# A Mamba prelude with fewer steps between the engines, and a side softmax that starts at step 5

## The reference, cut to what matters

```python
xs, z = split(u @ in_proj_w.T)                        # 256 + 256 channels
xs = silu(causal_conv4(xs, conv_w) + conv_b)          # 4 taps along the tokens
dt, B, C = split(xs @ x_proj_w.T, [64, 16, 16])
dt = softplus(dt @ dt_proj_w.T + dt_proj_b)
h = h * exp(dt * A) + (dt * xs) * B                   # a scan over the tokens, 16 states a channel
y = sum_over_states(h * C);  y = (y + D * xs) * silu(z);  out = y @ out_proj_w.T
```

## Time and profile before

| | us |
|---|---|
| median of three runs | 1351.88 |
| the three runs | 1352.38, 1351.88, 1346.26 |
| the profiled execution | 1346.07 |
| its span in the profile | 1344.3 |
| from the last block of X1 to the first drive | 62.63 to 154.72 |
| mean granted clock of PE over the span | 0.947 of full |

### The profile page before, as it was taken

How to read it: one execution, slowest core, us unless ns; L and a number is a source line. 1 busy time by engine, 2 the same in 40 slices (tenths; PEclk the granted TensorE clock), 3 DMA queues, 4 the chain that set the end, 5 groups by cost and what they waited for, 6 DMA issues and landing times.

```text
span 1344.3 us, 14496 instructions
## 1 busy us (share of the span) xinstructions
PE 1169.9 (87%) x4978; PEld 617.1 (46%) x4978; DVE 972.0 (72%) x1393; ACT 798.7 (59%) x1097; POOL 549.8 (41%) x291
## 2 busy tenths in 40 slices
PE   5677599999988798999658999999999999797888
PEld 1231144444433343444435666666566666432554
DVE  4557899999986435325668999999899999623353
ACT  4454666666645324222657888888888888534542
POOL 8000288888850655453002545445445454500000
PEclk8879599999998899999869999999999999998999
DMA  3000255555531211111000000000000000000000
GB/s 117 0 2 8 94 183 189 180 191 182 187 129 68 70 34 39 39 41 28 0 2 14 21 15 15 21 14 21 15 14 21 15 15 15 1 0 0 1 1 32
DMA packets 30825, 68.35 MB, mean 51 GB/s; under 512 B 6072, under 2 KB 11736, under 8 KB 30488
## 3 DMA queue, kind: packets, MB, share of 16 engines
q1 hardware_dynamic: 30752, 67.43, 15.4%
HBM read 65.18 MB, written 1.44 MB: 50 GB/s over the span
## 4 chain that ended last, share of the span: by engine, by line
DVE 38%; PE 38%; ACT 17%; issue 5%; POOL 1%; DMA 0%; DVEq 0%; POOLq 0%; SPq 0%; ACTq 0%
DVE work L585 10%; DVE work L1412 6%; DVE work L1431 5%; ACT ps L487 5%; PE ps L880 5%; PE ps L1066 4%; PE ps L896 3%; PE ps L888 3%; ACT work L1273 3%; DVE yd L1476 3%; ACT work L1268 3%; PE ps L1107 2%; DVE work L1479 2%; PE ps L1675 1%; PE ps L1575 1%
## 5 line engine op out<-in xcount | busy, mean ns | idle before, releaser
L1540 POOL TENSOR_TENSOR ssum<-ssum,rs 128x1024 f32<-128x1024 f32 x32 | 77.1, 2408 | 221.3 <-DVE work L1412 219.0
L585 DVE TENSOR_TENSOR_SCAN work<-ps,work 128x1024 f32<-128x1024 f32 x64 | 146.6, 2290 | 8.8
L605 POOL TENSOR_TENSOR work<-work 128x1024 f32<-128x1024 f32 x43 | 102.5, 2383 | 116.7 <-DVE work L585 116.7
L1412 DVE SCALAR_TENSOR_TENSOR work<-work,w_t 128x1024 f32<-128x1024 f32 x96 | 123.3, 1285 | 24.2 <-ACT work L1273 21.9
L870 POOL TENSOR_TENSOR work<-work,ssum 128x1024 f32<-128x1024 f32 x32 | 77.0, 2406 | 127.7 <-DVE work L955 79.3
L409 PE MATMUL ps<-work,ident 128*128 128x512 f32 x256 | 123.0, 604 | 2.5 <-POOL work L605 2.4
L955 DVE TENSOR_TENSOR work<-work,ps 128x512 f32<-128x512 f32 x64 | 43.9, 687 | 109.4 <-PE ps L888 109.2
L487 ACT ACTIVATE ps<-work,A 128x1024 f32<-128x1024 f32 x64 | 71.6, 1119 | 83.3 <-DVE work L585 81.8
L934 ACT ACTIVATE work<-ps 128x512 f32<-128x512 f32 x64 | 38.1, 597 | 131.2 <-PE ps L880 131.2
L1548 POOL TENSOR_TENSOR yd<-yd,work 128x896 f32<-128x896 f32 x32 | 67.1, 2096 | 69.7 <-DVE work L1479 69.7
L1455 DVE SCALAR_TENSOR_TENSOR work<-work,ps 128x64 f32<-128x64 f32 x384 | 79.3, 275 | 6.2
(11 more groups left out here) (342 smaller groups left out, 2604.4 us busy)
## 6 DMA issues: line engine op xcount, KB each, us to landing
work<-bc_rows SPq DMA_DIRECT2D x43, 512.0 KB, 3.6
yd<-bc_rows SPq DMA_DIRECT2D x21, 512.0 KB, 3.7
rs<-w_rows SPq DMA_DIRECT2D x32, 256.0 KB, 3.4
ssum<-share_rows SPq DMA_DIRECT2D x32, 256.0 KB, 3.0
w_t<-in_tile_w SPq DMA_DIRECT2D x32, 195.5 KB, 2.4
work<-in_w SPq DMA_DIRECT2D x1, 2048.0 KB, 8.0
shared<-in_f SPq DMA_DIRECT2D x3, 512.0 KB, 5.8
work<-in_x SPq DMA_DIRECT2D x4, 256.0 KB, 3.5
```

The source lines that it names most:

```text
L585: dve.tensor_tensor_scan(h, flat_pair(DABANK), h, 0.0, ALU.mult, ALU.add).then_inc(m0["scan"], 1)
L605: pool.tensor_tensor(HS[u % 4], HS[u % 4], CB[u % 3], ALU.mult).then_inc(m0["state"], 1)
L1412: c = dve.scalar_tensor_tensor(HC[u], HP[:, tap:tap + SEQ], par(u, "taps", tap), HC[u], ALU.mult, ALU.add)
L1540: pool.tensor_tensor(ssum[:, b, :], ssum[:, b, :], rs[:, :, :].rearrange("p k t -> p (k t)"), ALU.add).then_inc(m2["ss"], 1)
```

## The change

In the prelude: the peak of X1 is reduced block by block. The top-2 moves behind norm 2 (`f0_route_dve`), and its result is turned by 2 transposes instead of 16, evicted as 128x256, stored by SP in two DMAs (indicators and weights), and the indicators are loaded back. ACT writes the last tap of the convolution along with each eviction. `x_proj` is one product per block for dt, B and C. The bias of dt is a 65th row of `dt_proj` against a row of ones that POOL writes. Softplus is one function with its own table. POOL makes the middle and low parts of B. The four blocks go in two pairs, with the engines' lists interleaved. In the expert loop the plan `SOFT` is moved by `LAG` = 5 steps (5, 7, 9, 11, 15, 17, 19, 21), with all that hangs on it; gates(0), ups(0) and two gate blocks move too.

```diff
 def l0_clip_dve, per block k:
+    dve.wait_ge(m0["dve"], m0["x1"] + k + 1)
+    dve.tensor_reduce(gam[:, 0, 2 * k:2 * k + 2], blk(X1, k).rearrange("p (g t) -> p g t", t=GL), AX.X, ALU.max,
+                      apply_absolute_value=True).then_inc(m0["group_peak"], 1)
 def f0_dve, at its end:
-            top2(dve, own, rw[:, 0], rt[:, :, 0:E])
-            dve.tensor_tensor(rt[:, :, E:2 * E], rw[:, 0], rt[:, :, 0:E], ALU.mult).then_inc(f0["dve"], 1)
             l0_factor_dve(dve, own)
+        def f0_route_dve(dve, own):            # called after norm_dve(2)
+            dve.wait_ge(f0["dve"], f0["probs_out"] + 1)
+            top2(dve, own, rw[:, 0], rt[:, :, 0:E])
+            ind, w = (t.rearrange("p (e i) -> p i e", i=NT) for t in by_expert0)
+            dve.tensor_copy(ind, rt[:, :, 0:E])
+            dve.tensor_tensor(w, rw[:, 0], rt[:, :, 0:E], ALU.mult).then_inc(f0["dve"], 1)
 def l0_act, projection evictions:
+                        act.activation(pad[...], ps[:, 4 + m, :], ACT.Copy)
+                        act.activation(DL[:, MI * b + m, h * BL:(h + 1) * BL], ps[:, 4 + m, :], ACT.Identity,
+                                       scale=V("conv_w", m * DC + DC - 1), bias=V("conv_b", m)).then_inc(m0["act"], 1)
+            f0_turn_act(act)
+            gate_xs(0); gate_xs(1); low_out(0); low_out(1); gate_xs(2); rows_out(0); rows_out(1); gate_xs(3)
+            act.preload_act_table_set("softplus")
+            soft_plus(0); soft_plus(1); low_out(2); low_out(3); rows_out(2); rows_out(3)
+            soft_plus(2); soft_plus(3)
             act.preload_act_table_set("natural_log_exp_and_others")
+            def soft_plus(k):
+                act.wait_ge(m0["dtp"], k + 1)
+                act.activation(DL[:, MI * b:MI * (b + 1), h * BL:(h + 1) * BL], pair(4 + MI * (k % 2)), ACT.Softplus).then_inc(m0["delta"], 1)
 def l0_pe, after the projection:
+            f0_turn_pe(pe)
+            project_x(0); project_x(1); project_dt(0); project_dt(1)
+            project_x(2); project_x(3); project_dt(2); project_dt(3)
 def l0_dve, after norm_dve(2):
+            f0_route_dve(dve, own)
+            convolve(0); convolve(1); convolve(2); high_part(0); high_part(1); convolve(3)
+            high_part(2); high_part(3); step_x(0); step_x(1)
+            def high_part(k):
+                own(dve.tensor_copy(blk(parts[64:96, :], k), src))
+                if k >= 2:
+                    dve.wait_ge(m0["b_lo"], k - 1)
+                dve.tensor_tensor(bc_rest[:, k % 2, :], src, blk(parts[64:96, :], k), ALU.subtract).then_inc(m0["bc"], 1)
 def l0_pool:
+            pool.memset(dt_low[DR:DR + 1, :], 1.0).then_inc(m0["dt_ones"], 1)
+            for k in range(NB):
+                tb = part_tmp[0:32, k % 2, :]
+                pool.wait_ge(m0["bc"], k + 1)
+                own(pool.tensor_copy(tb, bc_rest[:, k % 2, :]))
+                pool.tensor_copy(blk(parts[32:64, :], k), tb)
+                pool.tensor_tensor(blk(parts[0:32, :], k), bc_rest[:, k % 2, :], tb, ALU.subtract).then_inc(m0["b_lo"], 1)
 SP, before it loads rows of C:
+            sp.wait_ge(m0["delta"], NB)
+            sp.wait_ge(m0["b_lo"], NB)
 expert loop:
-        SOFT = {j: 2 * j + 2 * (j // NB) for j in range(2 * NB)}
+        SOFT = {j: LAG + 2 * j + 2 * (j // NB) for j in range(2 * NB)}
-                if k == 1:
+                if k == NB - 2:
                     gates(0)
-                if k == 2:
+                if k == NB - 1:
                     ups(0)
-            pe.wait_ge(m1["dve"], m1["sub"] + 1)
-            l1_side_pe(pe, 0)
-                if n in (N1 - 4, N1 - 2):
+                if n in (N1 - 3, N1 - 1):
                     gate_block(...)
```

More of the change, by code:

```diff
@@ L203, in build @@
         norm = sems("norm", NORM)
[L204 to L207, removed]
+        m0 = stages("m0", pe="up:8 down:4 proj:16 outp:4",
+                    act="sign:3 biased:8 evac:16 sum_out:4",
+                    dve="weff:1 gated:8 x1:4 peak:1 scaled:4 ygate:4 s_out:4",
+                    each="gamma xd dtp group_peak dt_ones xs xd_out conv bc b_lo delta dtx b_mm c_out c_rows c_in0 c_in1 c_in2 ysum decay drive scan state")
         f0 = stages("f0", pe="logit:4 probs_T:1 picked_T:1 vT:1 mix:4", act="lg:4 exps:2 v_out:1 g:4",
-                    dve="top:2 probs:2 probs_out:1 picked:1 v:1 x_out:4", each="rt_out rows w_in0 w_in1 h1 h2 h3 r1 r2 r3 pooled summed")
+                    dve="top:2 probs:2 probs_out:1 picked:1 v:1 x_out:4", each="rt_out rows ind_in w_in0 w_in1 h1 h2 h3 r1 r2 r3 pooled summed")
         m1 = stages("m1", pe="logit:1 gq:2 gk:2 comb:2 s:4", act="exps:1 s_out:4",
@@ L374, in l0_pe, with project_x @@
                               start=True, stop=True).then_inc(m0["pe"], 1)
-            for k in range(NB):
+            f0_turn_pe(pe)
+            def project_x(k):
                 b, h = divmod(k, NB // BATCH)
-                pe.wait_ge(m0["act"], m0["xs"] + MI * (b + 1))
-                if k >= 2:
[L379 to L387, removed]
@@ new lines, in project_x, with project_dt @@
+                for m in range(MI):
+                    mm = pe.matmul(ps[0:DR + 2 * DS, k, :], W["x_proj"][:, m * (DR + 2 * DS):(m + 1) * (DR + 2 * DS)],
+                                   XS[:, MI * b + m, h * BL:(h + 1) * BL], start=(m == 0), stop=(m == MI - 1))
+                mm.then_inc(m0["xd"], 1)
+            def project_dt(k):
+                pe.wait_ge(m0["xd_out"], k + 1)
+                if k == 0:
+                    pe.wait_ge(m0["dt_ones"], 1)
+                    pe.wait_ge(m0["act"], m0["evac"] + 2 * MI * NB)
+                if k >= 2:
+                    pe.wait_ge(m0["delta"], k - 1)
+                for m in range(MI):
+                    mm = pe.matmul(ps[:, 4 + MI * (k % 2) + m, :], W["dt_proj"][:, m * P:(m + 1) * P], blk(dt_low, k), start=True, stop=True)
+                mm.then_inc(m0["dtp"], 1)
@@ L467, in l0_act @@
-            act.preload_act_table_set("natural_log_exp_and_others")
-            for k in range(NB):
-                for m in range(MI):
-                    n = MI * k + m
-                    act.wait_ge(m0["pe"], m0["dtp"] + n + 1)
-                    if n >= 2:
-                        act.wait_ge(m0["dve"], m0["delta"] + n - 1)
-                    t = tmp4[:, n % 2, :]
-                    own(act.activation(t, ps[:, 4 + n % 4, :], ACT.Abs, bias=V("dt_b", m)))
-                    own(act.activation(t, t, ACT.Exp, scale=-1.0))
-                    act.activation(t, t, ACT.Ln, bias=1.0).then_inc(m0["act"], 1)
@@ L571, in l0_dve @@
-            dve.wait_ge(m0["dve"], m0["delta"] + MI * NB)
-            dve.wait_ge(m0["pe"], m0["dtp"] + MI * NB)
-            for j in range(BATCH * MI):
-                dve.tensor_tensor(DX[:, j, :], DL[:, j, :], XS[:, j, :], ALU.mult).then_inc(m0["dve"], 1)
-            dve.wait_ge(m0["dve"], m0["dtx"] + BATCH * MI)
+                for i in range(DC - 1):
+                    c = dve.scalar_tensor_tensor(DL[:, j, :], pad[:, j, i:i + SEQ], V("conv_w", m * DC + i),
+                                                 DL[:, j, :], ALU.mult, ALU.add)
+                    if i < DC - 2:
+                        own(c)
```

170 lines of the change are left out of this document (93 added, 77 removed).

## The result

The changed kernel takes 1311.33 us (median of four runs, 1308.02 to 1315.25) against 1350.85 (four runs, 1346.26 to 1352.38) of the kernel before: ratio 0.9714, 95% interval 0.9678 to 0.9750. The forecast was 1316, range 1305 to 1331. The profiled execution took 1311.09 for a span of 1309.4, where before had 1346.07 and 1344.3: 34.9 us less in the span, against a forecast of 33.2.

The account below looks back on a forecast made before the run. No engine is full: the prelude is bound by engines handing blocks on, the expert loop by PE waits and low clock. 25.4 + 7.8 = 33.2 us gives 1312.9; halfway toward the median's 5.8 offset, 1316, range 1305 to 1331.

Parts of the forecast that it names:

- Steps 1 and 2: Prelude, X1 peak to factor: block reduces and top-2 off the path together gain 3.4 us (1.5 to 5.3).
- Step 1: Prelude, peak of X1: four reduces over 512 columns replace one over 2048; gain 1.6 us.
- Step 2: Prelude, top-2 off the path: factor then waits for POOL's all-reduce, starting at 66.8 (64.9 to 68.7) instead of 70.24.
- Step 3: Norm 2: transposes and table load out of the way gain 1.1 us, less 0.7 (0 to 2) for PE's low clock.
- Steps 4 to 7: Projection, convolutions, softplus, POOL and queues: first drive at 133.1 instead of 154.72, 21.6 us, including gains before the projection.
- The rule on the table load: ACT before softplus: a table switch of 2.66 us with drain would take 1.4 us more off the gain.
- The rule of exclusion: Prelude: fourth convolution's taps and step_x may each wait for POOL; 1 us taken on the path, 7.6 for six waits.
- Step 8: Expert loop, side softmax five steps later: 14.9 less 7.7 plus 0.6 for later gates, gain 7.8 us (5 to 10).
- Contention and clock eating a third: Prelude: all-reduce 1.9, norm 2 clock 1.3, projection clock 3, locks 6; gain 21, time 1325 to 1331; chance 0.17.
- The side shift empty: Expert loop: waits only moved, no gain there; total gain 25.4, time 1320 to 1326 us; chance 0.08.
- Softplus dear: Prelude on ACT: at three passes, four Softplus add 9 us, time 1325; chance 0.05.
- Slower by a low clock in the scan loop: Scan loop: over 10 units at low clock lose the whole gain, 15 units give 1365 us; chance 0.05.

Follow-up runs that it names:

- gates early: Changed kernel with gates(0) and ups(0) back where the kernel before has them; 1313.81 us, ratio 0.9743 to the kernel before.
- side back: Changed kernel with the expert loop as before (side softmax at steps 0, 2, 4, 6, old gate places); 1323.46 us, ratio 0.9823 to the kernel before.
- side only: Kernel before with only the expert-loop side part of the change, prelude untouched; 1339.89 us, ratio 0.9941 to the kernel before.
- side after gates: Changed kernel with each side product on PE behind the next step's gates products, ahead of its ups; 1296.96 us, ratio 0.9616 to the kernel before.
- POOL first: Changed kernel with one added 32x512 scratch product on POOL, ahead of MEMSET L632; 1316.84 us, ratio 0.9758 to the kernel before.
- parts on DVE: Changed kernel with the middle and low parts of B made on DVE instead of POOL; 1312.97 us, ratio 0.9748 to the kernel before.

## Why the prediction was right, and where its steps were off

The time and its place were as forecast: 27.5 us for 25.4 in the prelude, 6.4 to 9.8 for 7.8 in the expert loop. Step by step, in stage times, since X1 itself came 1.36 later. (With the new prelude X1 came at 62.6 in six traces and at 64.0 to 64.3 in six; both traces of the old one have 62.63. Whether the change has a part in this is open.)

*Steps 1 and 2.* 5.38 us for 3.4. Step 1 is exact: L551 ends 1.67 us after the update's start, L520 ended 3.27 after it, 1.60 less. Step 2 was mis-sized: 3.8 instead of 1.8. The all-reduce row, 0.39, was to be believed; I had gone half way to a bound that nothing supported.

*Step 3.* 1.07 (18.50 to 17.43) for a net 0.4. The 1.1 of gain was right. The 0.7 for a colder PE did not come: one variance pair runs at 2.08 behind 2.68 us of idle time, as one did before. Other traces of the same code have the pair at 2.08 elsewhere, and the stage stays between 17.42 and 17.64.

*Steps 4 to 7.* 65.98 to 44.94, 21.0 for 21.6. Each station up to the splits was 0.8 to 1.7 us sooner than I followed it through: first tap 9.8 us after the projection starts (forecast 10.6), fourth convolution done after 29.2 (30.9), splits after 37.9 (38.7). The first x_proj block took 3.4 us for my 2.9: I had called the pauses before the pairs of 1.12 and 2.08 alike, but they were 1.4 and 2.68 us. The 1 us for POOL beside the fourth convolution did not fall there: it took 3.93, since POOL was still in its 7.73 us before L638. It fell on step_x, which took 2.35 more, some 1.6 of it on the path. I had said that delta ends last. It is a tie: in the changed kernel the last Softplus ends 0.2 us before DVE is ready for it, in three of the six kernels with this prelude DVE waits 0.28 us for it. That the drive came out near the forecast (44.9 us after the projection's start for 44.4) is therefore in part luck, early stations against a dearer step_x. Softplus was 1.02 for the assumed 1.12. POOL's block is 2.44 us where DVE has only its casts and subtractions from PSUM, and 5.2 (122.23 to 127.46) beside step_x, around the 3.0 assumed; the C rows are out in time, as the product waits for the scan and not for its row:
```profile
132.21 2.35 POOL L644 TENSOR_TENSOR work<-work 128x1024 f32<-128x1024 f32 x1 [4.74 <-DVE work L616]
```

*The rule on the table load* (the Trainium skill, ScalarE: Activation LUTs, What ACT_TABLE_LOAD costs: 2.66 us with a drain) is not borne out: the silu L475 ends at 113.95, the load runs from 113.97 to 115.25, and Softplus starts at 115.26. The measurement decides: 1.28 and no drain.

*The rule of exclusion* between VectorE and GpSimd (the Trainium skill, SBUF — State Buffer, Who interferes with whom) agrees with where the microseconds went: 6.96 against 4.61 for step_x, 5.19 against 3.93 for the convolution. On the path step_x lost some 1.6 us by it, more than the 1 I took and far less than the 7.6 I named.

*Step 8.* The way to the first `outputs` takes 15.7 us for 30.4, at clock 1.00 (forecast 15.5). The moved side products wait 2.38 and 2.04, as assumed (2.10). Counted from gates(1), the way to the end of the first `outputs` is 15.8 us shorter and the rest of the stage 6.0 longer, for my 14.9 and 7.7. The 0.6 for the later gates did not show ("gates early"). The experts' gain is 9.83 or 6.4 according to the level at which the stage comes in that execution; that it has two I had not foreseen.

*The total.* The spans agree within 1.7 us. The median lies 4.7 under the forecast because I added 3 for the profiled execution of before being the fastest of its runs, and that of the changed kernel was a middle one.

*The rivals.* Contention and clock eating a third: of its four terms, 12.2 us together, the all-reduce (1.9) went the other way, the locks cost 1.6 on the path for 6, and the clock stays within the 1.9 us by which the same prelude varies, for 4.3. The side shift empty: refuted by "side back" and "side only". Softplus dear: 1.02. Slower by a low clock in the scan loop: the granted clock is 1.00 from 173 to 358, and the loop took 227.93 for 227.26.

*Left open:* why the untouched stages come at two levels. In the experts the clock goes with it, at X1 it does not, and no run here controlled the clock. Open too is how the 21.8 us of softplus, DX, x_proj and splits divide, but for the function, and "side after gates" was not joined with another edit.

## What to carry to other kernels

On an engine that works in order, look at what stands behind each waiting instruction: ready work of the length of the wait, put ahead of it, was worth 16 us here, more than the whole shift of five steps. Cut both traces into stages at the same instructions before explaining a difference, and compare an untouched stage over several executions before you trust 2 or 3 us in a touched one. Work handed to POOL is not free for DVE: count it where both read SBUF, and expect the wait to move to the next pair of operations when one of them is moved. A cost on an engine is not a cost on the path: ask what that engine would have waited for without it.

## What the hardware showed that was not expected

The first TENSOR_TENSOR on POOL starts 6.77 to 7.73 us after the operation ahead of it, in all eleven kernels in which it is a small one of the prelude (7.73 in the changed kernel, 6.77 in "POOL first"), while the MEMSET, CAST and COPY ahead of it start as soon as their inputs are there. In the kernel before and in "parts on DVE" POOL's first TENSOR_TENSOR is that of the scan loop, behind 91.9 and 33.8 us of idle time, and it starts within 0.1 us of the end of the scan that it waits for: such a cost does not show where POOL has long been idle. The Trainium skill (GPSIMD Engine Reference, 2.1 Instruction dispatch) has about 6 us for the first call of freshly loaded code; the traces come near it, 0.8 to 1.8 us longer, but that code is loaded there was not shown. Softplus costs no more than Exp or Ln of the same shape (1.02, 1.02, 1.06). POOL's own CAST and COPY of 0.60 us stretch to 1.60 and 1.49 beside DVE's products, so both sides pay.
